# Four graph layers in one kernel: the transformer's weighing done for pairs of blocks, with both operands split into a rounded and a remaining part

## The chip, the cores and the metric

The kernel runs on one core of a Trainium2 chip. The metric is the device time of one execution in microseconds (us), smaller is better. TensorE is called PE below, its weight loads PEld, VectorE DVE, ScalarE ACT, GpSimd POOL, and SyncE, which issues the transfers, SP.

## The reference

A graph has 3125 nodes with 128 features each and 100000 edges. Four residual layers follow one another: a sum over neighbours with a small network, a convolution, an attention with four heads, and a transformer of four layers. The change concerns the last of them:

```python
h = x @ Wn + bn
for l in range(N_LAYERS):                      # 4
    Q = h @ WQ[l] + bQ[l]; K = h @ WK[l] + bK[l]; V = h @ WV[l] + bV[l]
    scores = jnp.sum(Q[dst] * K[src], axis=-1) * scale
    seg_max = jax.ops.segment_max(scores, dst, num_segments=n)
    e = jnp.exp(scores - seg_max[dst])
    seg_sum = jax.ops.segment_sum(e, dst, num_segments=n)
    attn = e / seg_sum[dst]
    messages = jax.ops.segment_sum(attn[:, None] * V[src], dst, num_segments=n)
    out = messages @ WO[l] + bO[l]
    h = _layernorm(h + out, ln_g[l], ln_b[l])
return h @ Wout + bout                         # added to x
```

## The kernel before

The kernel treats the edges as a dense matrix. Its first half (up to 1683 us of the trace) builds a 3125 x 3125 matrix of edge counts and, from it, a bias that is the logarithm of a pair's count and hugely negative where there is no edge, and runs the first three layers. The change leaves this alone. The transformer takes the rest.

3125 nodes are 25 tiles or blocks of T = 125. A row of 3125 columns is cut in NC = 7 chunks, four of 500 columns (four tiles) and three of 375 (three tiles). In each of the four layers (`layer`, called in a loop of three and once more with names that hold `last`) there are three stages, each a block of code that all engines begin and end together.

Ahead: `K`, `Q` and `V` are made by PE. `K` is split in a rounded part `k_high` (type float32r) and the rest, `k_low`. DVE adds V's bias and writes `vals` (L1643), which has a column of ones behind the 128 features, so that the weighing also gives the sum of the weights.

The attention loop runs over 25 blocks of 125 queries. For each block and chunk:

- `scores` (L1742): three PE products of float32r operands, q_high with k_low, q_low with k_high, q_high with k_high, into one of three PSUM banks. POOL makes q_high and q_low of a block.
- `maximum` (L1815): DVE adds the bias rows of the block, which SP loads two blocks ahead (L1694, 1.6 MB each), writes the sum into `row` and takes its maximum; after seven chunks it takes the maximum of these (L1821).
- `exponential` (L1786): ACT, in place in `row`.
- `turn` (L1760): PE turns each tile of 125 x 125 into a PSUM bank, four or three tiles to a bank, three banks in turn (class `Turned`).
- `turned.copy`: ACT (chunks 1, 3, 5, L1134) or DVE (the others, L1136) copies the bank to `wcol`.
- `weigh` (L1751): PE multiplies the turned weights of a tile, as the stationary operand, with that tile of `vals`, 129 columns, in plain float32. In the trace such a product is two records.
- `finish`: DVE takes the reciprocal of the sum and writes the message, queries by features.

The order on each engine is written by hand in `step`: at chunk c PE does the scores of the chunk two further on (`ahead`), which after the last chunk is one of a later block, the turn of chunk c, and the weighing of chunk c - 1. ACT and DVE follow in the same order; DVE takes the maximum that is due before it copies.

Behind: PE turns the message (L657), ACT copies it to `cols`, PE multiplies it with WO, giving rows (L675), DVE adds h (L1891) and takes the statistics of the normalisation, and DVE and ACT apply them (L119, L115). In the last layer POOL also adds the output's bias to x within the loop. The last stage multiplies with Wout and adds x.

## Time and profile before

| | us |
|---|---|
| median of three runs | 3273.34 (3272.65 to 3277.59) |
| the profiled execution, its own time | 3271.98 |
| its span, first to last instruction | 3270.2 |
| mean granted PE clock, share of full | 0.929 |

| engine | busy us | share of the span | instructions |
|---|---|---|---|
| PE | 2689.7 | 82% | 21697 |
| PEld | 2261.5 | 69% | 21697 |
| DVE | 2249.2 | 69% | 4979 |
| ACT | 1676.1 | 51% | 2854 |
| POOL | 228.0 | 7% | 510 |

The attention loops of the four layers begin at 1719.5, 2109.8, about 2500 and 2893.6 us. All times within the trace count from the span's start. A line number is that of the code that issued an instruction; the copies of turned banks have those of a helper (L1134, L1136). In the timeline a row gives start, duration, engine, line, operation, what it writes and reads, and in brackets the engine's idle time before it and what ended it; rows marked x4 or x8 merge neighbours of one kind. Matmuls overlap: the time from one start to the next, the pitch, is what one costs, and its duration holds the time to its end as well.

### The profile page before, as it was taken

To read this page: it belongs to the slowest core of one execution; us is meant where nothing else is said; L and a number is where in the kernel's file an instruction comes from. 1 tells how busy PE (TensorE), PEld (TensorE's weight loads), DVE (VectorE), ACT (ScalarE), POOL (GpSimd) and SP (SyncE) were. 2 spreads that over 40 slices of the span, in tenths; PEclk is the share of its full clock that TensorE was granted. 3 is DMA by queue.
4 is the path that set the end of the run, shared out by engine and by line. 5 is a ranking of instruction groups with operands and counts; after the bars stand their busy time and mean duration, and the time that the engine had idled before them with its cause. 6 is when DMAs were issued, how large, how long until landed. Compare 5 with 4: busy or idle time off the path is not lost. (4 is left out here: it accounts for less than half of the span.)

```text
span 3270.2 us, 63722 instructions
## 1 busy us (share of the span) xinstructions
PE 2689.7 (82%) x21697; PEld 2261.5 (69%) x21697; DVE 2249.2 (69%) x4979; ACT 1676.1 (51%) x2854; POOL 228.0 (7%) x510
## 2 busy tenths in 40 slices
PE   1788888755588888888739999799997999889997
PEld 0555555544466666666628999699986999779997
DVE  8999999635499998999775555455545555545555
ACT  1666666512288887888733444444443444344443
POOL 3000000000000000000001110011101111011110
PEclk9999999877789998899869999999998999999999
DMA  1232322651432335232113332133322333133331
GB/s 40 90 121 107 123 106 106 245 145 61 124 130 102 119 121 169 104 118 100 64 45 122 117 117 101 63 118 117 117 81 86 119 120 119 53 112 119 120 121 40
DMA packets 87027, 351.76 MB, mean 108 GB/s; under 512 B 47396, under 2 KB 59484, under 8 KB 59739
## 3 DMA queue, kind: packets, MB, share of 16 engines
q1 hardware_dynamic: 86841, 349.39, 30.6%
q8 instruction: 104, 1.70, 0.2%
q14 instruction: 82, 0.66, 0.1%
HBM read 284.26 MB, written 64.07 MB: 107 GB/s over the span
## 5 line engine op out<-in xcount | busy, mean ns | idle before, releaser
L1815 DVE CUSTOM_DVE_ANT_0 l_arow<-l_scores,abias 125x500 f32<-125x500 f32 (+1 forms) x525 | 325.3, 621 | 368.3 <-issue 311.5
L1751 PE MATMUL l_asum<-vals,l_awcol 125*125 125x129 f32 x3750 | 516.3, 277 | 34.5 <-DVE l_awcol L1136 34.2
L1751 PEld LDWEIGHTS l_asum<-vals,l_awcol 125*125 125x125 f32 x3750 | 454.6, 187 | 61.7 <-DVE l_awcol L1136 52.8
L1404 PE MATMUL gturned<-ident,grow 125*125 125x125 f32 x2500 | 411.1, 306 | 29.0 <-ACT grow L1342 29.0
L1404 PEld LDWEIGHTS gturned<-ident,grow 125*125 125x125 f32 x2500 | 333.7, 205 | 107.0 <-issue 73.1
L1134 ACT ACTIVATE l_awcol<-l_aturned 125x500 f32<-125x500 f32 (+1 forms) x225 | 122.7, 545 | 516.5 <-PE l_aturned L1760 516.5
L1311 DVE SCALAR_TENSOR_TENSOR grow<-line,a_dst 125x3125 f32<-125x3125 f32 x100 | 347.6, 3476 | 34.9 <-DMA line<-lines_dram 25.3
L1786 ACT ACTIVATE l_arow<-l_arow,l_aneg 125x500 f32<-125x500 f32 (+1 forms) x525 | 323.2, 658 | 81.0 <-DVE l_aneg L1821 81.0
L1320 DVE CUSTOM_DVE_ANT_0 grow<-grow,bias 125x3125 f32<-125x3125 f32 x100 | 341.6, 3416 | 23.9 <-DMA bias<-bias_dram 9.7
L1342 ACT ACTIVATE grow<-grow,neg 125x3125 f32<-125x3125 f32 x100 | 290.4, 2904 | 122.2 <-DVE neg L1323 122.2
L1382 PE MATMUL gparts<-gwcol,h_mem 125*32 125x125 f32 x5000 | 245.6, 292 | 109.3 <-ACT gwcol L1355 109.3
L1760 PEld LDWEIGHTS l_aturned<-ident,l_arow 125*125 125x125 f32 x1875 | 280.6, 187 | 23.2
L1355 ACT ACTIVATE gwcol<-gturned 125x1000 f32<-125x1000 f32 x300 | 281.7, 1001 | 16.3 <-PE gturned L1404 16.2
L1760 PE MATMUL l_aturned<-ident,l_arow 125*125 125x125 f32 x1875 | 289.0, 271 | 0.0
L1382 PEld LDWEIGHTS gparts<-gwcol,h_mem 125*32 125x32 f32 x5000 | 133.7, 114 | 166.3 <-ACT gwcol L1355 72.3
L1742 PE MATMUL l_scores<-k_low,l_q_high 128*125 128x500 f32 (+1 forms) x525 | 234.7, 447 | 9.4 <-POOL l_q_low L1715 6.7
L449 DVE TENSOR_SCALAR hot_key<-iota_key,fixed 128x325 bf16<-128x325 f16 x1000 | 240.8, 311 | 0.3 <-issue 0.3
L503 PE MATMUL win<-hot_key,hot_place 128*125 128x325 bf16 x750 | 138.8, 305 | 121.7 <-DVE hot_key L449 101.1
L503 PEld LDWEIGHTS win<-hot_key,hot_place 128*125 128x125 bf16 x750 | 90.1, 137 | 188.1 <-DVE hot_key L449 84.4
L564 ACT ACTIVATE blk<-win 125x325 f32<-125x325 f32 x250 | 96.8, 445 | 198.0 <-PE win L514 197.9
L1815 DVE CUSTOM_DVE_ANT_0 l_last_arow<-l_last_scores,abias 125x500 f32<-125x500 f32 (+1 forms) x175 | 108.5, 621 | 128.1 <-issue 105.0
L1136 DVE COPY l_awcol<-l_aturned 125x500 f32<-125x500 f32 (+1 forms) x300 | 182.9, 610 | 19.8 <-PE l_aturned L1760 19.8
(320 smaller groups left out, 4549.9 us busy)
## 6 DMA issues: line engine op xcount, KB each, us to landing
abias<-bias_dram SPq DMA_DIRECT2D x100, 1562.5 KB, 6.5
bias<-bias_dram SPq DMA_DIRECT2D x50, 1562.5 KB, 6.5
bias_dram<-lnrow SPq DMA_DIRECT2D x25, 1562.5 KB, 5.2
counts_dram<-pair SPq DMA_DIRECT2D x13, 1562.5 KB, 6.5
pair<-counts_dram SPq DMA_DIRECT2D x13, 1562.5 KB, 16.4
line<-lines_dram SPq DMA_DIRECT2D x8, 1367.2 KB
fixed<-kp SPq DMA_DIRECT2D x250, 4.0 KB, 1.7
agg<-counts_dram SPq DMA_DIRECT2D x2, 1367.2 KB
```

The lines of the kernel that those rows point to most:

```text
L449: last = dve.tensor_scalar(hot_key[p][:, i, keys], G["iota_key"][:, keys], fixed[r][:, k, i, 0:1], base, ALU.subtract, ALU.is_equal)
L1311: dve.scalar_tensor_tensor(out=row[n % RING][:, :], in0=line[g][:, 0, :], scalar=a_dst[:, b, k:k + 1], in1=line[g][:, 1, :], op0=ALU.add, ...
L1320: dve.tensor_tensor_reduce(out=here, in0=here, in1=bias[i % 2][0:T, :], scale=1.0, scalar=-3.0e38, op0=ALU.add, op1=ALU.max, accum_out=top ...
L1342: act.activation(row[n % RING][:, :], row[n % RING][:, :], ACT.Exp, bias=neg[:, b, k:k + 1], accum_out=den[:, b, k:k + 1]).then_inc(exp_do ...
L1355: act.activation(wcol[q % RING][:, :].rearrange("p (g n) -> p g n", g=2), bank[q % RING][:, :, 0:C4], ACT.Copy).then_inc(col_copied, 1)
L1382: last = pe.matmul(part_ps[CH * j:CH * (j + 1), at:at + T], vals[:, t, k, :], wcol[q % RING][:, (t - t0) * T:(t - t0 + 1) * T], start=(t < ...
L1404: last = pe.transpose(bank[q % RING][:, j // 4, j % 4 * T:(j % 4 + 1) * T], row[n % RING][:, t * T:(t + 1) * T], ident[0:T, 0:T])
L1742: last = pe.matmul(s_ps[c % S_BANKS][:, 0:z - a], left[p][:, :], right[:, a:z], start=(n == 0), stop=(n == len(terms) - 1))
L1751: last = pe.matmul(sum_ps[p][:, :], wcol[c % T_BANKS][:, j * T:(j + 1) * T], vals[:, t, :], start=(t == 0), stop=(t == NT - 1))
L1760: last = pe.transpose(bank[c % T_BANKS][:, j * T:(j + 1) * T], row[p][:, t * T:(t + 1) * T], ident[0:T, 0:T])
L1786: act.activation(row[p][:, a:z], row[p][:, a:z], ACT.Exp, bias=neg[p][:, :]).then_inc(exp_done, 1)
L1815: dve.tensor_tensor_reduce(out=row[p][:, a:z], in0=s_ps[c % S_BANKS][:, 0:z - a], in1=bias[p][0:T, a:z], scale=1.0, scalar=-3.0e38, op0=AL ...
```

## The change

The weighing is done for two blocks of queries at once, and the operands change sides: the values are the stationary operand and the turned weights are moved past them. Both are split into a rounded part of type float32r and the rest. `vals_high` meets the 250 rounded weights and the 250 remaining ones of a tile (512 columns with padding), `vals_low` meets the rounded ones (256 columns). The sum comes as features by queries, in two halves of a bank, which ACT and DVE copy and add into `cols`, so the turning of the message in the stage behind falls away.

A pair of blocks goes in 13 units of two tiles: four turns to a bank (two tiles of two blocks). ACT copies each bank rounded, then DVE subtracts and writes the rest (`low_part`), and PE may weigh. Three things stand out: `first` does 17 chunks of scores and maxima ahead, `ahead` is three chunks instead of two, and the last block goes alone in seven units.

The column of ones goes: ACT's exponentials sum themselves (`accum_out`), DVE adds the seven sums (`den`), and in the stage behind takes the reciprocal, multiplies by `has_in`, and scales each tile in the addition of h. Four rows of weights are held instead of two; they lie in the memory of x, in `agg` and in two new tensors. x is therefore stored to DRAM at the start of the transformer, with the output's bias already added by DVE, and loaded again in the last stage behind the last loop.

```diff
-        vals = sbo("vals3", [T, NT, D + 1])
+        vals_high = sbo("vals_high", [T, NT, D], FP32R)
+        vals_low = sbo("vals_low", [T, NT, D], FP32R)
+        row = [x[:, :, :].rearrange("p t d -> p (t d)")[:, 0:N], agg[0:T, 0:N], *(sbo(f"arow{k}", [T, N])[:, :] for k in range(2))]
+        wcol = [sbo(f"awcol{k}", [T, 2, 2 * HALF], FP32R) for k in range(T_BANKS)]
...
                 def _(sp):
+                    sp.wait_ge(x_made, 1)
+                    load_rows(sp, G["x_dram"], x[:, :, :].rearrange("p t d -> p (t d)"), loaded)
...
                 def _(dve):
+                    dve.wait_ge(first_in, 16 * 3)
+                    dve.tensor_tensor(x[:, :, :], x[:, :, :], bout[:, :].unsqueeze(1).broadcast_to([T, NT, D]), ALU.add).then_inc(x_made, 1)
...
+                            for c in range(NC):
+                                act.wait_ge(v_made, c + 1)
+                                act.activation(vals_high[:, part, :], spare[:, part, :], ACT.Copy).then_inc(v_rounded, 1)
...
+                            def low_values(c):
+                                dve.wait_ge(v_rounded, c + 1)
+                                dve.tensor_tensor(vals_low[:, part, :], spare[:, part, :], vals_high[:, part, :].bitcast(FP32),
+                                                  ALU.subtract)
                             for c in range(NC):
-                                dve.tensor_tensor(vals[:, ts[0]:ts[-1] + 1, 0:D], rows_view(bank, c, D),
+                                dve.tensor_tensor(spare[:, ts[0]:ts[-1] + 1, :], rows_view(bank, c, D),
...
+                                dve.wait_ge(v_made, c + 1)
+                                dve.sem_inc(banks.read["dve"], 1)
+                                if c:
+                                    low_values(c - 1)
+                            low_values(NC - 1)
...
+                    def ahead(P, e, u, act_on):
+                        for k in ((0, 1) if u == 0 else (u + 1,)):
+                            g = k + AHEAD
+                            to, f = (P + 1, 1 - e) if g < PAIR_CHUNKS else (P + 2, e)
+                            half, c = divmod(g % PAIR_CHUNKS, NC)
+                            if exists(to, half):
+                                act_on(to, f, half, c)
...
+                            def turn(P, e, u):
+                                pe.wait_ge(exp_done, (2 * P + halves - 1) * NC + (chunk_of(ts[-1]) + 1))
...
+                                for j, t in enumerate(ts):
+                                    for half in range(halves):
+                                        at = (halves * j + half) * T
+                                        last = pe.transpose(turned_ps[slot(P, e, u)][:, at:at + T], row[2 * e + half][:, t * T:(t + 1) * T], ident[0:T, 0:T])
+                                last.then_inc(turned_ready, 1)
+
+                            def weigh(P, e, u):
...
+                                pe.wait_ge(low_made, P * UNITS + (u + 1 + UNITS))
+                                wide = HALF if single(P) else 2 * HALF
+                                for j, t in enumerate(tiles(P, u)):
+                                    terms = ((vals_high, wide), (vals_low, HALF))
+                                    for n, (left, n_cols) in enumerate(terms if t == 0 else terms[::-1]):
+                                        last = pe.matmul(sum_ps[e][:, 0:n_cols], left[:, t, :], buffer[:, j * wide:j * wide + n_cols],
+                                                         start=(t == 0 and n == 0), stop=(t == NT - 1 and n == 1))
...
+                            def step(P, e):
+                                for u in units(P):
+                                    if not single(P):
+                                        ahead(P, e, u, scores)
+                                    turn(P, e, u)
+                                    if u:
+                                        weigh(P, e, u - 1)
+                                weigh(P, e, units(P)[-1])
...
+                                act.activation(row[k][:, a:z], row[k][:, a:z], ACT.Exp, bias=neg[k][:, :],
+                                               accum_out=expsum[k][:, c:c + 1]).then_inc(exp_done, 1)
...
+                            def step(P, e):
+                                for u in units(P):
+                                    act.wait_ge(turned_ready, P * UNITS + (u + 1 + 2 * UNITS))
+                                    act.activation(operand(P, e, u, 0), turned(P, e, u), ACT.Copy).then_inc(high_copied, 1)
+                                    if u == 1 and not (isinstance(P, int) and P == 0):
+                                        finish(P - 1, 1 - e)
...
+                                    for c in ((u + 2,) if u < 3 else (5, 6) if u == 3 else ()):
+                                        exponential(P, e, 1, c)
+                                    if 4 <= u < 4 + NC:
+                                        exponential(P + 1, 1 - e, 0, u - 4)
+                                    if u >= 4 + NC and exists(P + 1, 1):
+                                        exponential(P + 1, 1 - e, 1, u - 4 - NC)
...
+                            def low_part(P, e, u):
+                                dve.wait_ge(high_copied, P * UNITS + (u + 1))
+                                dve.tensor_tensor(operand(P, e, u, 1), turned(P, e, u), operand(P, e, u, 0).bitcast(FP32), ALU.subtract
+                                                  ).then_inc(low_made, 1)
+
+                            def finish(P, e):
+                                for half in range(1 if single(P) else 2):
+                                    dve.wait_ge(exp_done, b * NC + NC)
+                                    dve.tensor_reduce(den[:, bass.ds(b, 1)], expsum[k][:, :], AX.X, ALU.add)
+                                dve.wait_ge(msg_high, P + 1)
+                                dve.tensor_tensor(here, here, sum_ps[e][:, at:at + wide], ALU.add).then_inc(sum_read, 1)
+
+                            def step(P, e):
+                                for u in units(P):
+                                    if not single(P):
+                                        ahead(P, e, u, maximum)
+                                    low_part(P, e, u)
+                                    if u == 2 and not (isinstance(P, int) and P == 0):
+                                        finish(P - 1, 1 - e)
+                            first(maximum)
...
                         def _(pe):
-                            pe_turn(pe, banks, "msg", msg, D, ident)
-                            banks.done(pe, "msg")
                             pe_rows(pe, banks, "out", [cols], [w[:, 3, :]])
...
                         def _(act):
-                            act_columns(act, banks, "msg", cols)
                             norm.root(act)
...
                         def _(dve):
+                            chain(dve, m, dve.reciprocal(den[:, :], den[:, :]))
+                            chain(dve, m, dve.tensor_tensor(den[:, :], den[:, :], G["has_in"][:, :], ALU.mult))
...
-                                    dve.tensor_tensor(work[:, part, :], rows_view(bank, c, D), h[:, part, :], ALU.add).then_inc(banks.read["dve"], 1)
+                                    for j, t in enumerate(ts):
+                                        end = dve.scalar_tensor_tensor(out=work[:, t, :], in0=bank[0:T, j * D:(j + 1) * D], scalar=den[:, t:t + 1],
+                                                                       in1=h[:, t, :], op0=ALU.mult, op1=ALU.add)
+                                    end.then_inc(banks.read["dve"], 1)
```

## Rows read from the trace of the kernel before

**Rows 1.** The windows view, the loop of layer 1; busy us and instructions, then PE's clock.

```profile
core 0: us, PE busy (x) PEld busy (x) DVE busy (x) ACT busy (x) POOL busy (x), PEclk, DMA share, GB/s
1718.00:2060.00 342.00, 327.24 (x2401) 305.20 (x2401) 179.81 (x525) 140.20 (x251) 39.73 (x100) 1.00 0.31 109
```

**Rows 2.** The page's costliest groups: the weight loads of the weighing.

```profile
L1751 PEld LDWEIGHTS l_asum<-vals,l_awcol 125*125 125x125 f32 x3750 | 454.6, 187 | 61.7 <-DVE l_awcol L1136 52.8
```

**Rows 3.** The timeline, PE, one unit of the loop in layer 1.

```profile
1906.31 0.60 PE L1760 MATMUL l_aturned<-ident,l_arow 125*125 125x125 f32 x4
1906.63 0.96 PEld L1751 LDWEIGHTS l_asum<-vals,l_awcol 125*125 125x125 f32 x8
...
1906.74 1.05 PE L1751 MATMUL l_asum<-vals,l_awcol 125*125 125x129 f32 x8
...
1907.55 0.42 PE L1742 MATMUL l_scores<-k_low,l_q_high 128*125 128x376 f32 x1
...
1907.80 0.33 PE L1742 MATMUL l_scores<-k_high,l_q_low 128*125 128x376 f32 x1
...
1907.98 0.33 PE L1742 MATMUL l_scores<-k_high,l_q_high 128*125 128x376 f32 x1
...
1908.14 0.60 PE L1760 MATMUL l_aturned<-ident,l_arow 125*125 125x125 f32 x4
```

**Rows 4.** The timeline: the last score product of 500 columns, turns, ACT's copy.

```profile
1904.02 0.39 PE L1742 MATMUL l_scores<-k_high,l_q_high 128*125 128x500 f32 x1
...
1904.25 0.60 PE L1760 MATMUL l_aturned<-ident,l_arow 125*125 125x125 f32 x4
...
1904.88 0.59 ACT L1134 ACTIVATE l_awcol<-l_aturned 125x500 f32<-125x500 f32 x1 [4.80 <-PE l_aturned L1760]
```

**Rows 5.** The timeline: a block's last unit, where PE waits.

```profile
1900.14 0.49 PE L1760 MATMUL l_aturned<-ident,l_arow 125*125 125x125 f32 x3
...
1900.48 0.68 DVE L1815 CUSTOM_DVE_ANT_0 l_arow<-l_scores,abias 125x500 f32<-125x500 f32 x1 [0.99 <-issue]
...
1901.08 0.54 DVE L1136 COPY l_awcol<-l_aturned 125x375 f32<-125x375 f32 x1
...
1901.68 0.93 PE L1751 MATMUL l_asum<-vals,l_awcol 125*125 125x129 f32 x6 [0.39 <-DVE l_awcol L1136]
```

**Rows 6.** The timeline of ACT: a copy that sums, in the first half; exponentials.

```profile
416.33 0.59 ACT L577 ACTIVATE crow<-turn 125x500 f32<-125x500 f32 x1
416.79 0.21 ACT L577 ACTIVATION_READ_ACCUMULATOR crow<-turn 125x1 f32 x1
416.88 0.69 ACT L578 ACTIVATE lnrow<-turn,tiny 125x500 f32<-125x500 f32 x1
...
1911.22 1.31 ACT L1786 ACTIVATE l_arow<-l_arow,l_aneg 125x500 f32<-125x500 f32 x2 [0.86 <-DVE l_aneg L1821]
```

**Rows 7.** The timeline: stages behind the loop of layer 1 and ahead of the next.

```profile
2059.99 2.86 PE L657 MATMUL l_attn_out_bank<-ident,agg 125*128 125x125 f32 x25 [0.98 <-PEq L1687]
...
2063.86 5.72 PE L675 MATMUL l_attn_out_bank<-w,cols 128*125 128x128 f32 x50 [1.00 <-ACT cols L684]
...
2076.18 3.93 DVE L119 TENSOR_SCALAR h_mem<-work,stat 125x128 f32<-125x128 f32 x15 [0.15 <-DVE stat L106]
...
2102.97 0.69 DVE L1643 TENSOR_TENSOR vals<-l_qkv_bank,rows 125x512 f32<-125x512 f32 x1 [4.85 <-PE l_qkv_bank L675]
```

**Rows 8.** The timeline: the loop's start in layer 1 and in the last layer.

```profile
1719.52 0.49 PE L1742 MATMUL l_scores<-k_low,l_q_high 128*125 128x500 f32 x1 [2.24 <-POOL l_q_low L1715]
...
1720.76 0.68 DVE L1815 CUSTOM_DVE_ANT_0 l_arow<-l_scores,abias 125x500 f32<-125x500 f32 x1 [2.88 <-PE l_scores L1742]
...
1727.24 0.60 PE L1760 MATMUL l_aturned<-ident,l_arow 125*125 125x125 f32 x4
...
2893.56 0.78 PE L1742 MATMUL l_last_scores<-k_low,l_last_q_high 128*125 128x500 f32 x1 [7.02 <-POOL l_last_q_low L1715]
...
2902.54 0.60 PE L1760 MATMUL l_last_aturned<-ident,l_last_arow 125*125 125x125 f32 x4
```

**Rows 9.** The page's part on transfers: the bias rows, us from issue to landing.

```profile
abias<-bias_dram SPq DMA_DIRECT2D x100, 1562.5 KB, 6.5
```

245 lines of the change are left out of this document (111 added, 134 removed).

## The prediction

> **What bounds the kernel now.** I read the page's first two parts, then the windows by stage, then one unit of the attention loop in the timeline, since the change touches nothing ahead of the transformer. The windows show that in the loop over the 25 blocks of queries PE is busy for 327 of 342 us, its weight loads for 305, DVE for 180 and ACT for 140, and that its clock is granted in full, 2.4 GHz [rows 1]. The loop runs four times. In layer 1 it goes from the first score at 1719.52 to the end of the last block; the next PE work starts at 2059.99, so a layer's loop is 340.5 us, 7.7 of it ahead of the first turn at 1727.24 [rows 7, 8], and a block takes (340.5 - 7.7)/25 = 13.3 us.
>
> A unit of four tiles and 376 score columns lasts 1.83 us, from turn at 1906.31 to turn at 1908.14. Four turns take 0.43; eight weighing products (two a tile, since the operands are plain float32) take 0.81; a score product of 376 columns takes 0.17 to the next, one of 500 columns 0.23 (1904.02 to 1904.25) [rows 3, 4]; over several I read 0.171 and 0.227. So a turn is 0.108 us, a weighing tile 2 x 0.108. A block is 75 x 0.108 + 12 x 0.227 + 9 x 0.171 = 12.36 us of PE; the 13.3 leave 0.95 of gaps. The largest is at the last unit: DVE takes a maximum first, so its copy ends late and PE waits 0.39 [rows 5]. PE's own work sets the loop's time.
>
> **Weighing, the main term.** Two blocks now share one product. Per tile the rounded values meet 512 columns (both blocks, rounded and remaining part) and the remaining part of the values meets 256. Both are of the scores' type, whose pitch is 0.227 at 500 columns and 0.171 at 376, that is 0.45 ns a column: 0.232 at 512 and 0.117 at 256, 0.349 a tile. A pair of blocks falls from 100 x 0.108 = 10.8 to 25 x 0.349 = 8.7 us. Turns (50 x 0.108 = 5.4) and scores (8.5) stay. PE work of a pair: 22.6. The weight load of the next product must hide behind the 256-column one: the loads last 187 ns, but eight of them take 0.96, so they follow one another at 0.11 [rows 2, 3], hidden behind products of 0.108 now; so I cost them nothing; without that cover see rival 2.
>
> **The way from turn to weighing.** Today one engine copies a turned bank. Now ACT copies it rounded, DVE then subtracts and writes the rest, and PE waits for DVE. From the turns' last slot: 0.16 to their end (four turns last 0.60, their slots 0.43), 0.03 to ACT's start (1904.85 to 1904.88), 0.59 ACT, 0.03, 0.68 DVE (a sum of 512 from PSUM with a second operand lasts 0.69), 0.06 to PE as at 1901.62: 1.55 us [rows 4, 5, 7]. PE meanwhile weighs the unit before (0.70), scores (0.51 or 0.68) and turns (0.43): 1.64 to 1.81. The way is covered by 0.1 to 0.25, a thin cover. Gaps of a pair: the last unit has one tile, so 0.22 + 0.70 stands against a maximum (it starts 0.34 after the scores' last slot, 1900.14 to 1900.48, and takes 0.60 [rows 5]) and 0.46 for low part and signal, 0.5; the closing of the former pair on DVE (two sums of 0.16, one addition of about 0.4) shortly after the maximum's reduction, 0.3; the 0.03 a unit loses today, 0.4; the two double chunks, 0.3. Sum 1.5 us, between 0.5 (only the last unit) and 2.0 (today's, 2 x 0.95). A pair takes 24.1.
>
> **ACT and DVE.** ACT's exponentials now sum as well. Where ACT reads its accumulator today, the next instruction starts 0.09 after the read (416.79, 416.88), and a copy with its read takes 0.55, where a copy alone lasts 0.59 and overlaps its successor by 0.1 [rows 6, 4]; two exponentials last 1.31, so they follow at 0.61. A pair: 14 exponentials 9.1, 13 copies 6.2, closing 0.3: 15.6 of 24.1. DVE: 14 maxima 7.8, reductions 0.6, 13 subtractions 7.7, closing 0.7: 16.8 of 24.1. Neither is the bound. Behind DVE's new wait for ACT's copy stands the next maximum, and behind that PE's scores three chunks later; DVE is idle for a third of a unit, so nobody waits. Behind ACT's wait for the finished sum (unit 1) stand exponentials needed from unit 2 on, and the sum was finished a unit before.
>
> **The loop's ends.** Before the first turn now come 19 chunks of scores instead of 10, the 15th of which needs the bias rows of block 2. SP issues that load when the first chunk of block 1 has been read: first maximum 1.24 after the first score [rows 8], seven maxima about 4.2, one more 0.7, issue at 6.3; landing 6.5 later [rows 9], 12.8; one maximum, two chunks of scores: first turn at 14.8 instead of 7.7, with 9 x 0.61 = 5.5 of work moved ahead. The eleven full pairs take 265.1. In the pair before the last only four chunks of scores are left (2.1), PE has 16.2 of work and the way of 1.55 stands bare against 1.13 in ten units (4.2): 21.3 with the odd gap. The single block: 25 x (0.108 + 0.234) = 8.6 and seven gaps of 0.2, 10.0, then 0.7 for the sum's end. Loop: 14.8 + 265.1 + 21.3 + 10.7 = 311.9. That is 28.6 less than 340.5.
>
> **Ahead of the loop.** DVE adds V's bias at 0.69 a bank [rows 7], paced by PE at 0.875. Now each bank has a second operation of about 0.62, and the first must end before its bank is given back (0.05): 4 x 1.36 + 3 x 1.1 = 8.7 instead of 5.1 us, ACT's rounding hidden beside it. +3.7. The loop waits for it. PE idles for 6 us there instead of 2.2; in the last layer, where it idles 7.02, its first product lasts 0.78 instead of 0.49, which is the level of 1.2 GHz, and its first turn comes 8.98 after the first score instead of 7.72 [rows 8]. I take +1.2 for three layers (0 to 1.2).
>
> **Behind the loop.** 25 turns of the message and ACT's copies go: 2059.99 to 2063.86, -3.9. DVE's addition of h becomes 25 products with a column instead of 7 wide sums (priced like V's, 0.60 and 0.48 in pitch): 15 such operations on 128 columns took 3.93, 0.26 each [rows 7], up to 0.3 from PSUM, so 6.9 against 3.8, +3.1. The reciprocal of the sums and one product, on 25 columns each, fit before the first bank, 1 us after PE starts. Together -0.8, between -2 and +1.
>
> **Free of cost.** The addition of the output bias to x (3.5 us of DVE) lies in the node stage, where DVE waits while PE turns h and multiplies columns; SP's store of x waits for it, lands in about the 6.5 of an equally large load [rows 9], and that stage has 11 us left; SP has nothing queued behind. The reload of x lies beside 25 us of the last normalisation and costs 7 if that cover fails. GpSimd's memsets have 15 us. GpSimd's 25 additions to x go, off the path; its start in the last layer waits for four loads instead of five, perhaps -0.4, left out.
>
> **The sum.** Per layer -28.6 + 3.7 - 0.8 = -25.7, four times -102.8, and 3 x 1.2 = +3.6: -99.2. The profiled execution took 3271.98 (span 3270.2), 1.4 under the median of the three runs, 3273.34; from the median: 3174.
>
> **Rivals.** (1) The way through two engines sets the pace: PE turns the next unit only in name, and a bank's stay, 0.43 + 0.16 + 0.03 + 0.59 + 0.03 + 0.68 = 1.92, becomes the unit: 13 x 1.92 = 25.0 and 0.5 at the last, 25.5 a pair, +1.4 x 11.5 x 4 = +64, 3238. For it: the cover is only 0.1 thick and ACT, DVE have an order written out by hand. Against: three banks turn round, so a bank may stay for three units. The Trainium skill ("Trainium Kernel Development and Optimization", Best Practices) warns that speeding up TensorE does not speed up the emptying of PSUM; by that rule the change, which reads each bank twice, would end at this rival. The trace's 140 and 180 busy us of ACT and DVE leave room that the rule does not count, hence a low chance: 0.17.
> (2) The change does not do what it says: the product of 256 columns costs its weight load, 0.187 instead of 0.117, as PE can't hide a load behind so short a product of this type. +0.07 x 25 x 48 = +84, 3258. For it: no row has such a product. Against: loads of the same width follow at 0.11 in weighing [rows 3]. 0.10.
> (3) Slower: DVE's subtraction comes in behind a maximum that has just begun, and waits for 0.69 and the 0.17 of its start. The way becomes 1.55 + 0.86 = 2.41, and with one turn ahead the unit is half of 2.41 + 1.72 (PE's mean work), 2.07: a pair 27.4 with 0.5 at its end, +3.3 x 11.5 x 4 = +152, 3326. It is slower than before once a unit passes 1.98. For it: just this happens today at the last unit, where the copy waits for the maximum's end [rows 5]. Against: in other units the maximum is released 0.4 before the turn and ends 0.25 before ACT's copy. 0.07.
> (4) Gaps shrink to 0.5 a pair and the clock holds: -46 - 4, 3124. 0.12.
>
> **Chances.** Forecast 0.54 (3145 to 3210), the rivals as given. A measurement of this kernel can tell 0.2% (6.5 us) from no change. Faster 0.90, same 0.02, slower 0.08: rival 3, and the tail of 2. The range of 8 in 10 takes in rivals 1 and most of 4, and stops at rival 2's centre: 3128 to 3252.
>
> **What would show it.** Weighing at 0.232 and 0.117 in pitch, or 0.19 for the short one (rival 2). A unit of 1.64 to 1.85 with PE's idle time at weighing under 1.5 a pair, or PE waiting in each unit for DVE's low part (1, 3). First turn 14 to 15 us after the first score, DVE waiting there for the bias load. V's stage longer by 3 to 4, the stage behind shorter by 1. ACT and DVE busy 65% and 70% of the loop. Wrong would be the forecast if ACT's read of its accumulator costs its full 0.2 us in the exponentials (14 x 0.11 more, 17.1 of 24.1, still hidden, but unit 3 with two of them would stall), or if layers differ by more than the clock's 1.2.

## The result and the profile after

The changed kernel takes 3186.84 us (median; 3177.73 to 3191.4) against 3272.99 for the kernel before on the same chip: ratio 0.973, 95% interval 0.971 to 0.976, 86 us less. The forecast was 3174. The profiled execution took 3186.86, span 3185.1, 85.1 us shorter than the span before.

The windows view of the new kernel, over the loop of layer 1 (busy us and instructions by engine, then PE's clock), answers to [rows 1]:

```profile
core 0: us, PE busy (x) PEld busy (x) DVE busy (x) ACT busy (x) POOL busy (x), PEclk, DMA share, GB/s
1719.00:2030.00 311.00, 291.92 (x1742) 257.04 (x1740) 223.59 (x575) 207.86 (x523) 40.16 (x100) 0.99 0.34 120
```

PE is still busy for nearly the whole loop. DVE rose from 180 of 342 us to 224 of 311 (72%), ACT from 140 to 208 (67%).

The timeline of the new kernel, one unit (four turns, four weighing products, a chunk of scores, the next turns), answers to [rows 3, 4]:

```profile
1853.12 0.27 PE L1771 MATMUL l_aturned<-ident,agg 125*125 125x125 f32 x1
...
1853.15 0.36 PE L1783 MATMUL l_asum<-awcol,vals_low 125*128 125x256 f32 x1
...
1853.35 0.39 PE L1783 MATMUL l_asum<-awcol,vals_high 125*128 125x512 f32 x1
...
1853.43 0.59 ACT L1822 ACTIVATE awcol<-l_aturned 125x500 fp32r<-125x500 f32 x1 [0.55 <-PE l_aturned L1771]
1853.58 0.28 PE L1783 MATMUL l_asum<-awcol,vals_low 125*128 125x256 f32 x1
...
1853.70 0.40 PE L1783 MATMUL l_asum<-awcol,vals_high 125*128 125x512 f32 x1
...
1853.93 0.33 PE L1755 MATMUL l_scores<-k_low,l_q_high 128*125 128x376 f32 x1
...
1854.05 0.68 DVE L1862 TENSOR_TENSOR awcol<-l_aturned,awcol 125x500 fp32r<-125x500 f32 x1 [0.22 <-ACT awcol L1822]
...
1854.45 0.27 PE L1771 MATMUL l_aturned<-ident,x 125*125 125x125 f32 x1
```

The wide weighing product costs 0.23 (1853.35 to 1853.58, and 1853.70 to 1853.93), the short one 0.12 (1853.58 to 1853.70), to the next product's start. ACT's copy starts 0.04 after the last turn's end, DVE's subtraction 0.03 after the copy's, and it ends at 1854.73, when PE still has its turns to finish.

The pairs can be counted off by the one copy of the finished sum that ACT makes in each. The timeline of the new kernel, ACT alone, copies of pairs 1, 10, 11 and of the last block:

```profile
1771.96 0.38 ACT L1817 ACTIVATE cols<-l_asum 128x250 f32 x1
...
2013.77 0.38 ACT L1817 ACTIVATE cols<-l_asum 128x250 f32<-128x250 f32 x1
...
2032.17 0.38 ACT L1817 ACTIVATE cols<-l_asum 128x250 f32<-128x250 f32 x1
...
2041.87 0.28 ACT L1817 ACTIVATE cols<-l_asum 128x125 f32<-128x125 f32 x1 [1.65 <-PE l_asum L1783]
```

From the first to the second of these lie ten pairs: 24.18 us each.

To compare layers I take four marks from the timeline of each kernel: GpSimd's first operation of a layer, the first score, the first turn, and PE's first work behind the loop. In us, layers 1 to 4 (the last "behind" runs to the final stage's first product):

| stretch | before | after | change, all four |
|---|---|---|---|
| ahead: to the first score | 18.5, 23.3, 23.2, 25.1 | 22.7, 29.2, 29.0, 28.7 | +19.6 |
| first score to first turn | 7.7, 7.7, 9.2, 9.0 | 18.0, 17.1, 17.3, 16.8 | +35.6 |
| first turn to the loop's end | 332.8, 332.8, 333.0, 332.7 | 297.3, 297.4, 298.2, 298.1 | -140.3 |
| behind | 26.5, 26.4, 26.4, 24.4 | 25.2, 25.2, 25.1, 23.1 | -5.2 |

They add up to -90.3. The final stage has +1.4 and the unchanged first half of the program +3.8 in this execution; together -85.1. That first half varies: with the same code the first layer began between 1694.6 and 1715.1 us in the profiles below. Where an effect is small I therefore compare the time from the first layer's start to the end of the span: 1569.2 us before, 1480.3 after.

The timeline of the new kernel, the start of layer 1's loop, answers to [rows 8]:

```profile
1727.49 0.78 PE L1755 MATMUL l_scores<-k_low,l_q_high 128*125 128x500 f32 x1 [6.45 <-POOL l_q_low L1730]
1728.07 0.62 PE L1755 MATMUL l_scores<-k_high,l_q_low 128*125 128x500 f32 x1
1728.49 0.62 PE L1755 MATMUL l_scores<-k_high,l_q_high 128*125 128x500 f32 x1
...
1729.40 0.68 DVE L1852 CUSTOM_DVE_ANT_0 x<-l_scores,abias 125x500 f32<-125x500 f32 x1 [3.50 <-PE l_scores L1755]
...
1736.46 8.15 SPq L1709 DMA_DIRECT2D abias<-bias_dram  x2
...
1743.43 0.68 DVE L1852 CUSTOM_DVE_ANT_0 arow<-l_scores,abias 125x500 f32<-125x500 f32 x1 [3.39 <-DMA abias<-bias_dram]
...
1744.17 0.50 PE L1755 MATMUL l_scores<-k_low,l_q_high 128*125 128x500 f32 x1 [2.64 <-DVE l_atop L1852]
```

PE has idled for 6.45 us and its products follow at 0.42, not 0.23; DVE waits 3.39 us for block 2's bias rows, PE 2.64 for DVE. The granted clock of the first four microseconds says why the products are slow (windows view, new kernel):

```profile
1705.00:1715.00 10.00, 10.00 (x27) 4.98 (x28) 4.41 (x7) 7.63 (x13) 0.22 (x1) 1.00 0.83 322
...
1727.00:1731.00 4.00, 3.51 (x9) 2.80 (x10) 1.15 (x3) 0.74 (x1) 1.79 (x5) 0.50 0.29 68
```

Half of full speed, that is 1.2 GHz, after 6.45 us without work. The first four microseconds of the four loops were granted 0.50, 0.50, 0.51 and 0.59 in the new kernel, and 1.00, 1.00, 0.59 and 0.63 in the kernel before, where PE had idled 2.24, 2.25, 2.25 and 7.02.

In layers 3 and 4 the level fell once more behind the first turn (windows view, new kernel, the first 24 us from the first turn of layers 1 to 4):

```profile
1745.50:1769.50 24.00, 23.18 (x142) 20.64 (x141) 17.16 (x43) 16.38 (x41) 3.87 (x10) 1.00 0.52 192
2114.30:2138.30 24.00, 23.19 (x142) 20.63 (x141) 17.16 (x43) 16.38 (x41) 3.89 (x10) 1.00 0.53 191
2483.20:2507.20 24.00, 23.72 (x138) 21.36 (x137) 17.16 (x43) 16.49 (x41) 3.88 (x10) 0.93 0.50 180
2852.00:2876.00 24.00, 23.72 (x138) 21.42 (x138) 17.29 (x43) 16.48 (x41) 3.91 (x10) 0.93 0.49 178
```

These are the two loops that took 298.2 and 298.1 us in the table, some 0.8 more than the others.

The return from one layer to the next looks different too. The timeline of the new kernel, layer 2, answers to [rows 7]:

```profile
2068.01 0.45 POOL L1589 TENSOR_TENSOR rows<-rows 125x128 f32<-125x128 f32 x1 [72.17 <-POOLq L1956]
2068.23 2.70 SPq L1585 DMA_DIRECT2D abias<-bias_dram  x2
2071.05 0.15 DVE L1612 TENSOR_SCALAR bq<-bq 128x1 f32<-128x1 f32 x1 [8.01 <-issue]
...
2071.89 4.54 PE L665 MATMUL l_qkv_bank<-cols,w 128*128 128x500 f32 x5 [7.06 <-issue]
```

PE begins 3.9 us behind GpSimd, and the profile names nothing that it waited for. In the kernel before it began 0.2 behind.

### The profile page after: what moved, and what is told of

It reads as the page before. It is cut to its first block and busy times, and to the rows that moved or that the text cites. A ratio compares the mean times of both kernels' runs of the same rounds, so it can differ in the third digit from the quotient of the medians.

```text
span 3185.1 us, 60275 instructions
## 1 busy us (share of the span) xinstructions
PE 2573.7 (81%) x19197; PEld 2090.7 (66%) x19197; DVE 2451.7 (77%) x5292; ACT 1956.1 (61%) x3958; POOL 221.1 (7%) x487
## 5 line engine op out<-in xcount | busy, mean ns | idle before, releaser
L1822 ACT ACTIVATE awcol<-l_aturned 125x500 fp32r<-125x500 f32 (+2 forms) x489 | 279.2, 572 | 290.8 <-PE l_aturned L1771 288.8
L1365 PE MATMUL gturned<-ident,grow 125*125 125x125 f32 x2500 | 410.3, 306 | 29.2 <-ACT grow L1303 29.2
L1862 DVE TENSOR_TENSOR awcol<-l_aturned,awcol 125x500 fp32r<-125x500 f32 (+2 forms) x489 | 321.2, 657 | 109.9 <-ACT awcol L1822 102.1
L1365 PEld LDWEIGHTS gturned<-ident,grow 125*125 125x125 f32 x2500 | 332.8, 204 | 107.5 <-issue 73.0
L1783 PE MATMUL l_asum<-awcol,vals_high 125*128 125x512 f32 (+1 forms) x975 | 360.1, 390 | 19.0 <-DVE awcol L1862 19.0
L1281 DVE CUSTOM_DVE_ANT_0 grow<-grow,bias 125x3125 f32<-125x3125 f32 x100 | 341.7, 3417 | 24.4 <-DMA bias<-bias_dram 10.2
L1783 PE MATMUL l_asum<-awcol,vals_low 125*128 125x256 f32 x975 | 305.0, 322 | 13.5 <-DVE awcol L1862 12.9
L1316 ACT ACTIVATE gwcol<-gturned 125x1000 f32<-125x1000 f32 x300 | 282.0, 1002 | 19.2 <-PE gturned L1365 19.1
L1755 PE MATMUL l_scores<-k_low,l_q_high 128*125 128x500 f32 (+1 forms) x525 | 201.3, 383 | 27.5 <-POOL l_q_low L1730 19.3
L1783 PEld LDWEIGHTS l_asum<-awcol,vals_high 125*128 125x128 f32 x975 | 184.7, 189 | 43.2 <-DVE awcol L1862 18.8
L1852 DVE CUSTOM_DVE_ANT_0 arow<-l_scores,abias 125x500 f32<-125x500 f32 (+1 forms) x252 | 154.8, 622 | 74.5 <-PE l_scores L1755 56.8
L1783 PEld LDWEIGHTS l_asum<-awcol,vals_low 125*128 125x128 f32 x975 | 184.8, 190 | 31.8 <-DVE awcol L1862 30.0
L1755 PE MATMUL l_scores<-k_high,l_q_low 128*125 128x500 f32 (+1 forms) x525 | 194.0, 369 | 0.0
L1755 PE MATMUL l_scores<-k_high,l_q_high 128*125 128x500 f32 (+1 forms) x525 | 193.9, 369 | 0.0
```

The costliest lines, as they stand in the source:

```text
L1281: dve.tensor_tensor_reduce(out=here, in0=here, in1=bias[i % 2][0:T, :], scale=1.0, scalar=-3.0e38, op0=ALU.add, op1=ALU.max, accum_out=top ...
L1316: act.activation(wcol[q % RING][:, :].rearrange("p (g n) -> p g n", g=2), bank[q % RING][:, :, 0:C4], ACT.Copy).then_inc(col_copied, 1)
L1365: last = pe.transpose(bank[q % RING][:, j // 4, j % 4 * T:(j % 4 + 1) * T], row[n % RING][:, t * T:(t + 1) * T], ident[0:T, 0:T])
L1755: last = pe.matmul(s_ps[g % S_BANKS][:, 0:z - a], left[half][:, :], right[:, a:z], start=(n == 0), stop=(n == len(terms) - 1))
L1783: last = pe.matmul(sum_ps[e][:, 0:n_cols], left[:, t, :], buffer[:, j * wide:j * wide + n_cols], start=(t == 0 and n == 0), stop=(t == NT ...
L1822: act.activation(operand(P, e, u, 0), turned(P, e, u), ACT.Copy).then_inc(high_copied, 1)
```

## The experiments

My theory after reading: PE's own work sets the loop, the way over ACT and DVE is just covered, and the 13 us that the forecast missed lie at the seams (the bias wait, the stage ahead, the return to a layer's begin) and in the first half. The rivals: the way sets the unit; ACT or DVE is a bound; one of the seams is not what it seems. All edits are to the changed kernel, except where the heading names the kernel before.

**PE's work less: weighing without the values' remaining part.**

```diff
-  for n, (left, n_cols) in enumerate(terms if t == 0 else terms[::-1]):
+  for n, (left, n_cols) in enumerate(terms[:1]):
```

> Weighing keeps only the product of the rounded values; the product with the values' remaining part (256 columns, 0.117 us a tile) is left out, so the messages lack that part. My theory: PE's own work sets the unit, with a way from turn to weighing of 1.58 us just covered. Without two such products a unit has 1.49 of work; with one turn ahead it can't fall under (1.49 + 1.58)/2 = 1.53, so it goes from about 1.76 to 1.50 to 1.53: 2.3 to 2.9 us a pair, 46 pairs: 106 to 135 us less, some 3065 us. Rival (the way over ACT and DVE sets the unit, as a bank's stay of 1.9): 0 to 10 us less, 3180. Rival (the load of the next weights is not hidden behind the short product and costs 0.187): more than 150 less.

Measured: 3089.4 us, ratio to the kernel before 0.943 (0.939 to 0.946). From the transformer's start to the end 1383.9 instead of 1480.3, 96 less, where I expected 106 to 135. A pair takes 22.21 instead of 24.18 (ACT's copies of the sum, 1773.42 to 1995.50 for ten): -1.97, under the -2.3 expected. The time does follow PE's work, so the way alone is no bound; but the saving is 2.9 of PE's work and only two thirds of it came through. The timeline of this run, DVE with ACT's copies and one weighing product, says where it stops:

```profile
1877.26 0.68 DVE L1862 TENSOR_TENSOR awcol<-l_aturned,awcol 125x500 fp32r<-125x500 f32 x1 [0.22 <-ACT awcol L1822]
...
1878.06 0.68 DVE L1852 CUSTOM_DVE_ANT_0 arow<-l_scores,abias 125x500 f32<-125x500 f32 x1
...
1878.22 0.59 ACT L1822 ACTIVATE awcol<-l_aturned 125x500 fp32r<-125x500 f32 x1 [0.41 <-PE l_aturned L1771]
...
1878.85 0.68 DVE L1862 TENSOR_TENSOR awcol<-l_aturned,awcol 125x500 fp32r<-125x500 f32 x1
...
1880.67 0.51 PE L1783 MATMUL l_asum<-awcol,vals_high 125*128 125x512 f32 x1 [0.36 <-DVE awcol L1862]
```

DVE now goes from subtraction to maximum to subtraction with a gap of 0.22 or none. PE's waits for DVE in layer 1's loop rose from 27.1 us (60 times) to 35.0 (74 times) though PE had less to do. These rows suggest that DVE, together with the way, comes next, some 2 us a pair under today's; DVE was busy 208 of 272 us of this loop, so it isn't full, and no run parts the two.

**The way longer: ACT copies half of each bank once more.**

```diff
+  once = turned(P, e, u)[:, :, 0:T] if not single(P) else turned(P, e, u)
+  if u or not isinstance(P, int) or P:
+      act.wait_ge(high_copied, P * UNITS + u)
+  act.activation(extra[:, 0:once.shape[1], :], once, ACT.Copy)
   act.activation(operand(P, e, u, 0), turned(P, e, u), ACT.Copy).then_inc(high_copied, 1)
```

> ACT copies half of each turned bank (250 columns; all of it in the last block) once more, into a buffer of its own, ahead of its copy: the way from turn to weighing grows by about 0.38 us, PE's work stays. My theory (covered way, unit = the larger of PE's 1.72 and half of PE's 1.72 plus the way, now 1.96): a unit goes from 1.76 to about 1.84, 12 x 0.08 + 0.38 at the last unit = 1.3 us a full pair, 44 pairs; the pair before the last and the single block, where the way stands bare, +4.6 and +3.9 a layer: about +90 us in all, 3275. Rival (the way or the bank's stay is the unit): 0.38 x 12.5 x 46 = +220 us, 3405. Rival (a cover as wide as the three banks would allow, 1 us): only the bare places, +50.

Measured: 3300.3 us, ratio 1.007 (1.005 to 1.010): 115.6 us more from the transformer's start on, nearer to my +90 than to +220 or +50. The added copy lasted 0.38. A pair takes 26.38, +2.2 where I had +1.3, and the pair before the last 21.70 instead of 18.40. PE's waits for DVE in layer 1's loop more than doubled in number:

```profile
1880.39 0.38 ACT L1827 ACTIVATE extra<-l_aturned 125x250 f32<-125x250 f32 x1
...
1880.58 0.50 PE L1784 MATMUL l_asum<-awcol,vals_high 125*128 125x512 f32 x1 [0.81 <-DVE awcol L1868]
```

They are 57.3 us, 129 times, of 163 units. A kernel with 0.38 us more in the way is 0.7% slower than the one before the change: the cover is real and thin. The model (a unit is half of the way plus PE's work once the way is longer than PE's work) gives the right kind of answer and is 0.9 a pair low.

**The way shorter: DVE subtracts and writes half of each bank.**

```diff
-  dve.tensor_tensor(operand(P, e, u, 1), turned(P, e, u), operand(P, e, u, 0).bitcast(FP32), ALU.subtract
+  half = T if not single(P) else T // 2
+  dve.tensor_tensor(operand(P, e, u, 1)[:, :, 0:half], turned(P, e, u)[:, :, 0:half],
+                    operand(P, e, u, 0)[:, :, 0:half].bitcast(FP32), ALU.subtract
```

> DVE subtracts and writes only the first half of each bank's remaining part (the rest of it is left out of the result): the way is 0.3 us shorter, PE's work the same, DVE has 3.7 us less a pair. My theory (PE sets the unit): only the bare places gain, 0.3 x (11 last units + 12 units of the pair before the last + 7 of the single block) = 9 us a layer, 36 in all if every one of them is bare, 20 if half are: 3150 to 3167 us. Rival (the way sets the unit): 0.3 x 12.5 x 46 = 172 less, 3015. Rival (it doesn't matter at all): within 6 us of the changed kernel.

Measured: 3156.6 us, ratio 0.964 (0.961 to 0.967); 28.1 less from the transformer's start on. A pair takes 23.78 (-0.40, the last unit's gap and a little), the pair before the last 16.99 (-1.4). (DVE also has 3.7 us less to do in a pair here; this run doesn't part that from the shorter way.) The three runs fit together: PE's work less by 2.9 a pair gives 2.0; the way shorter by 0.3 a unit gives 0.4 a pair; the way longer by 0.38 a unit costs 2.2 a pair. In the changed kernel PE's work sets the full units and the way only the places where there is less work beside it.

**No sums in the exponentials.**

```diff
-  act.activation(row[k][:, a:z], row[k][:, a:z], ACT.Exp, bias=neg[k][:, :],
-                 accum_out=expsum[k][:, c:c + 1]).then_inc(exp_done, 1)
+  act.activation(row[k][:, a:z], row[k][:, a:z], ACT.Exp, bias=neg[k][:, :]).then_inc(exp_done, 1)
...
-  dve.tensor_reduce(den[:, bass.ds(b, 1)], expsum[k][:, :], AX.X, ALU.add)
```

> The exponentials no longer sum and DVE no longer adds up the partial sums (the division by the sums of weights is left out: divisor 1). My theory: ACT has a third of its time free, the 14 reads of its accumulator a pair (0.09 us each in pitch) and DVE's two reductions lie beside PE's work: 0 to 10 us less, of which the start of each layer's loop may give 1. Rival (ACT is the bound in the units with two exponentials, or DVE at the closing of a pair): 14 x 0.09 x 46 = 58 us less, 3129.

Measured: 3183.0 us, ratio 0.971 (0.968 to 0.974), and 1479.8 from the transformer's start against 1480.3. The sums of weights cost nothing that this measurement can tell.

**Block 2's bias loaded at the layer's start.**

```diff
+  sp.dma_start(row[2], G["bias_dram"][2, 0:T, :]).then_inc(bias2_in, 16)
...
+  added = row[2] if isinstance(P, int) and P == 1 and half == 0 else bias[half][0:T, :]
-  ... in1=bias[half][0:T, a:z],
+  ... in1=added[:, a:z],
```

(SP's loop leaves out its own load of that block.)

> The bias rows of block 2 are loaded at the layer's start into the buffer in which that block's scores with bias are written (free by then), so the 15th chunk of scores need not wait for a load that is issued after block 0 is read. My theory: DVE waited 3.4 us for that load in every layer, and PE with it; first turn 14.5 instead of 17.9 us after the first score, 4 x 3.4 = 14 us less, 3173 us. Rival (something else is as late, DVE's 19 maxima or ACT's 9 exponentials): under 1 us a layer, under 4 in all. Rival (three loads of 1.6 MB at the layer's start collide with what the first chunks need): no gain or a loss.

Measured: 3169.2 us, ratio 0.968 (0.966 to 0.970); 13.8 less from the transformer's start on. The first turn came 15.0, 14.3, 14.2 and 14.4 us after the first score, 11.4 less over the four layers, so most of the wait came back. Another 1.8 came in the loops of layers 3 and 4, which now took 297.3 and 297.2 us: the clock stayed at 1.00 over the first 24 us behind their first turns, where it had been 0.93.

**V made first.**

```diff
+  pe_rows(pe, banks, "v", [cols], [w[:, 2, :]])
   pe_columns(pe, banks, "k", w[:, 1, :], cols)
   pe_columns(pe, banks, "q", w[:, 0, :], cols)
-  pe_rows(pe, banks, "v", [cols], [w[:, 2, :]])
```

(ACT and DVE follow: V's rounding and bias first, five of the seven subtractions of V between those of K.)

> In the stage of the projections PE makes V first, then K and Q, so that DVE splits V beside PE's products for K and Q and not behind them; the work is the same. My theory: DVE's work of this stage is 14 x 0.65 + 7 x 0.74 = 14 us and bounds it only if it begins late; first score 18.5 to 19.5 us after PE's first product instead of 22.6, 3 to 4 us a layer, and PE idles less ahead of the scores, so that its clock stays at the upper level: another 0 to 1. 12 to 20 us less in all, 3170 us. Rival (ACT with 21 copies, or the block's end and GpSimd's staging, takes over): 0 to 4 less.

Measured: 3173.1 us, ratio 0.969 (0.967 to 0.971); 10.8 less from the transformer's start on, 2.7 a layer instead of 3 to 4 and more. The timeline of this run, the first score of layer 1:

```profile
1719.01 0.50 PE L1756 MATMUL l_scores<-k_low,l_q_high 128*125 128x500 f32 x1 [2.21 <-POOL l_q_low L1731]
1719.35 0.39 PE L1756 MATMUL l_scores<-k_high,l_q_low 128*125 128x500 f32 x1
```

PE's idle time is back at 2.21 us and the first products follow at the upper level, 0.34 and 0.23, but not for long: the first four microseconds of the four loops were granted 0.58, 1.00, 0.67 and 0.50. Of the clock's share little came back, and the short idle time alone doesn't keep the level. The first score comes 20.6 us after PE's first product instead of 22.6: PE waits for DVE within the stage now (0.76 and 0.35 in layer 1), and ACT waits for PE's products for Q.

Layer 2 of this run shows the new kernel's chain at the upper level: block 2's load was issued 6.7 us after the first score, DVE waited 3.38 us for it, and the first turn came at 15.7. In layers 1, 3 and 4, with the low level in the first four microseconds, the issue came at 8.1 to 8.9 and the first turn at 16.8 to 17.9.

**The same, by GpSimd.** V last as in the changed kernel, with GpSimd subtracting instead of DVE.

> The same stage with V last as in the changed kernel, but GpSimd makes V's remaining part, with DVE left to add the bias. An addition of 128 columns on GpSimd takes 0.45 us in this trace; no row shows one of 512. If it takes 1.0: first score 3 us earlier, 12 less in all. If it takes 1.6 (the length of four small ones without their start): 7 x 1.6 = 11 us against V's 6.1, no gain, 0 to +10.

Measured: 3189.6 us in one run, +2.8 from the transformer's start on. The timeline of this run, GpSimd:

```profile
1717.73 7.82 POOL L1594 TENSOR_TENSOR vals_low<-agg,vals_high 125x512 fp32r<-125x512 f32 x7 [12.71 <-ACT vals_high L1614]
```

Seven subtractions in 7.8 us: 1.27 for one of 512 columns and 0.99 for one of 384, between my two cases. The first score came only 0.1 earlier, since the last of them ends at 1725.55. What I had left out is that the seven take longer than PE's 5.6 for V, and that the chain (DVE's addition, ACT's rounding, GpSimd) also starts 2.5 us behind PE's first product for V.

**More code in a layer.**

```diff
   step(0, 0)
-  with eng.Fori(0, (LAST_PAIR - 2) // 2) as i:
+  step(1, 1)
+  step(2, 0)
+  with eng.Fori(1, (LAST_PAIR - 2) // 2) as i:
```

> Pairs 1 and 2 of each layer are written out instead of running in the loop: the same work, more instructions in a line. In layers 2 and 3 PE's first product stands 3.9 us behind GpSimd's start, waiting for nothing that the profile shows. Theory (instructions are fetched by DMA after the jump back to the layer's begin, and the more of them the program has the later they come): the wait at that place stays at 3.9 or grows, and new waits of the same kind appear inside the layer; 0 to +15 us. Rival (it is the bias loads that slow the stage's start): unchanged, 3.9, and total within 3 us.

Measured: 3176.3 us in one run, 1477.9 from the transformer's start on (-2.4). PE's wait at the return was 7.13 and 6.75, against 7.06 and 6.93, with 1037 matmuls in the code of a repeated layer instead of 753: it doesn't grow with the code.

**The bias loads later.**

```diff
   def _(sp):
+      sp.wait_ge(banks.filled, 1)
       for p in range(2):
           sp.dma_start(bias[p][:, :], G["bias_dram"][p, :, :]).then_inc(bias_in[p], 16)
```

> SP issues the two bias loads of a layer's start only when PE has filled its first bank, so that nothing else uses the DMA engines while PE's first instructions of the layer come. Theory (PE's start in layers 2 and 3 is late because its instructions are fetched by DMA and share the engines with 3.1 MB of bias): PE's wait before its first product falls from 7.0 to about 3.3 us, 7 us less in all. Rival (the fetch is late by itself, from the jump back on): the wait stays at 6.5 to 7.2 us.

Measured: 3183.9 us in one run, 1480.0 from the transformer's start on. The timeline of this run:

```profile
2068.70 3.70 PE L665 MATMUL l_qkv_bank<-cols,w 128*128 128x500 f32 x4 [6.94 <-issue]
...
2070.77 0.84 SPq L1586 DMA_DIRECT2D abias<-bias_dram  x2
```

With the loads issued 2.1 us behind PE's start, the wait is as long as ever (6.94 and 6.91). The bias loads are not its cause.

**The kernel before, with more code in a layer.**

```diff
-  with eng.Fori(0, NT // 2 - 1) as i:
+  with eng.Fori(0, 8) as i:
       step(2 * i, 0)
       step(2 * i + 1, 1)
-  for b in range(NT - 3, NT):
+  for b in range(16, NT):
```

> The kernel before, with blocks 16 to 21 of each layer written out instead of running in the loop: the same work, but 1059 matmuls stand in the code of a repeated layer instead of 633 (792 in the run without the values' remaining part, where PE began layers 2 and 3 without delay; 917 in the changed kernel, where it was 3.9 us late). Theory (the jump back to the layer's begin costs PE a fetch of instructions once its code for a layer is longer than something between 792 and 917 matmuls): PE's idle time before its first product in layers 2 and 3 rises from 3.3 to about 7 us, with the wait put down to issue, and the total by 7 to 8 us. Rival (it is something else in the changed kernel): 3.3, as in the kernel before.

Measured: 3270.6 us in one run, 1571.0 from the transformer's start on, against 1569.2. The timeline of this run:

```profile
2083.02 0.45 POOL L1615 TENSOR_TENSOR rows<-rows 125x128 f32<-125x128 f32 x1 [63.09 <-POOLq L1903]
...
2086.53 1.20 PE L665 MATMUL l_qkv_bank<-cols,w 128*128 128x500 f32 x1 [6.58 <-issue]
```

The wait is there (6.58 and 6.37 instead of 3.3), made by nothing but code written out: the late start belongs to the length of a layer's code. The expectation's counts are each 164 too high. The code of a repeated layer holds 469 matmuls in the kernel before, 628 without the values' remaining part, 753 in the changed kernel (39 for the projections, 51 ahead of the first turn, 142 for each of three pairs, 112 and 75 for the last two, 50 behind) and 895 here. So the limit lies above 628 and at most at 753.

The transfers of the profile show what goes with it. The part on transfers, changed kernel, layer 2 (2068 to 2437 us):

```profile
q8 instruction: 9, 0.15, 0.2%
```

Nine blocks of 16 KB came in on a queue that the profile names instruction, the first at 2069.0, 1.0 us behind GpSimd's first operation and 2.9 ahead of PE's first product. The run with more code has 11 of them in each of layers 2 and 3, this run 12. The kernel before and the run without the values' remaining part have none there, after 5 and 6 in layer 1, and in them PE is on time. So PE starts late where a layer's instructions are brought in anew at each repetition.

But it costs little. From GpSimd's first operation to the first score it is 24.0 us instead of 23.2 in both layers, since the kernel before has a stall of the same kind on DVE at that place, which the later start covers (timeline, kernel before):

```profile
2089.42 0.74 DVE L1637 SCALAR_TENSOR_TENSOR k_low<-l_qkv_bank,bq,k_high 128x500 fp32r<-128x500 f32 x1
...
2094.45 3.66 DVE L1637 SCALAR_TENSOR_TENSOR k_low<-l_qkv_bank,bq,k_high 128x500 fp32r<-128x500 f32 x6 [4.30 <-issue]
```

The run without the values' remaining part has the same: PE begins on time in layers 2 and 3, then waits 3.2 and 3.4 us for DVE, which is held up for 4.9 us (put down to issue), and the first score comes 28.0 and 29.6 us after GpSimd's first operation, against 29.2 and 29.0 in the changed kernel, where PE begins late: on average 0.3 apart. So my total of +7 to +8 was wrong while the wait was right, and I had read the wait as if all of it were a loss.

What does lengthen this stretch is the clock. The windows view over the 5.3 us from PE's first product on, first the changed kernel in layer 2, then the run without sums in layer 3, whose stage is the same:

```profile
2071.89:2077.19 5.30, 5.30 (x7) 2.32 (x8) 1.48 (x2) 1.35 (x2) 0.00 (x0) 0.50 1.01 419
...
2437.98:2443.28 5.30, 5.30 (x9) 2.38 (x10) 1.11 (x2) 2.16 (x4) 0.00 (x0) 0.71 1.00 417
```

At 0.50 the first score came 29.2 us after GpSimd's first operation, at 0.71 28.0.

**Both gains together.** Bias ahead and V first.

> Both edits that took time off: block 2's bias loaded at the layer's start, and V made first. By the traces of the two alone, the first turn came 2.7 us earlier after the first score in layers 1 to 4 with the one (15.0, 14.3, 14.2, 14.4 against 18.0, 17.1, 17.3, 16.8), and the first score 2.0, 1.1, 2.0, 2.8 us earlier after PE's first product with the other. If they add up: 11 + 8 = 19 to 24 us less than the changed kernel, ratio to the kernel before 0.9665 to 0.968. Rival (the two share a cover, since with V first the loads land later in relation to the scores): no better than the better one alone, 0.9677.

Measured: 3164.7 us, ratio to the kernel before 0.965 (0.962 to 0.968), below the changed kernel's interval of 0.971 to 0.976; 1456.3 from the transformer's start on, 24.0 less, where the two alone have 13.8 and 10.8. They add up. The first turn comes 14.4, 12.8, 12.8 and 15.2 us after the first score. The windows view of the first four microseconds of this run's loops in layers 2, 3 and 1:

```profile
2099.30:2103.30 4.00, 3.98 (x19) 3.23 (x19) 2.73 (x9) 0.28 (x1) 2.26 (x6) 1.00 0.29 63
2461.50:2465.50 4.00, 4.00 (x19) 3.24 (x20) 2.78 (x9) 0.23 (x1) 2.26 (x6) 1.00 0.27 59
1735.80:1739.80 4.00, 4.00 (x11) 3.21 (x12) 1.41 (x5) 0.24 (x1) 1.95 (x5) 0.57 0.36 82
```

With the same code and the same 2.2 us of idle time, the low level costs 1.6 us of this stretch (14.4 against 12.8). This is the fastest kernel of the study that computes the whole result.

## Why the prediction came out as it did

The time fell inside the range and 13 us above its centre; the mechanism was the one forecast.

- **Weighing.** 0.232 and 0.117 were read off the scores' pitch and stand in the trace, the short product as well. Rival 2 is out: the next weights' load hides behind 256 columns.
- **The pair and the loop.** 24.1 forecast, 24.18 measured; eleven pairs 266.0 (1745.48 to the turn at 2011.49) against 265.1. The pair before the last took 19.1, not 21.3, and the single block 12.2, not 10.7 (turns at 2011.49 and 2030.59, end at 2042.79). The first was costed as if the way stood bare in every unit, the second with gaps of 0.2 where PE idles up to 1.05; the two errors happen to cancel. First turn to the loop's end: 297.1 forecast, 297.3 in layer 1. All four: -140.3 against -142.8; 1.8 of the difference lie in layers 3 and 4, where the clock fell again behind the first turn.
- **The way.** 1.55 forecast; from the turns' last slot at 1853.23 to 1854.81 it is 1.58. Rivals 1 and 3 are out: in eleven full pairs of 13 units PE waits for DVE's part 43 times, 20.9 us in all, 1.9 a pair where the sum had 1.5 of gaps; in most units it doesn't wait, and DVE has finished its maximum and waits for ACT (0.22 in the unit above), not the other way round. What was said for rival 1, the thin cover, was right about its size (0.38 more made the kernel slower than before the change).
- **The Trainium skill's rule.** The Trainium skill ("Trainium Kernel Development and Optimization", Best Practices) says that "TensorE tiling speeds up compute but not PSUM evacuation", which the prediction took for a faster PE of any kind. Today's full units show little of it: with the way 0.3 a unit shorter a pair gained 0.4 of 24.2, and 28 us came back in all, in good part at the last units and the last pairs. The run with 2.9 us less PE work a pair, which gained 2.0, shows more of it.
- **Behind the loop.** -0.8 a layer forecast, -1.3 measured: eight products with a column took 2.16 from PSUM, 0.27 each, and DVE was otherwise covered as said.
- **Ahead of the loop.** +3.7 a layer forecast; +4.2 in layer 1, +5.9 in layers 2 and 3, +3.6 in the last. The extra 1.7 of layers 2 and 3 lies at the return to the layer's begin, a seam that I had not looked at. The run with the longer code before gives 0.7 of it for the same late start. The other 1.0 fits the clock: it stood at the low level for 5.3 us behind PE's start, against some 3 in the kernel before, and runs of the same stage in which that was some 3 too took 28.0 to 28.2 instead of 29.2.
- **First score to first turn: the mis-sized term.** 14.8 forecast, 18.0 measured in layer 1. The chain was right (block 2's bias, issued after block 1's first maximum, then one maximum, two chunks of scores), its first link was not: the issue came 9.0 us after the first score, not 6.3. PE was at 1.2 GHz, so that the first maximum began 1.91 after the first score instead of 1.24 and the first four followed at 1.1 to 1.25 instead of 0.6. The landing took 6.8, not 6.5, and DVE went on 0.2 later. At the upper level (V made first, layer 2) the issue came at 6.7 and the first turn at 15.7, so of the 3.2 us that layer 1 missed by some 0.9 are the chain itself and the rest goes with the clock.
- **The clock.** I gave it 1.2 in three layers, as a price of its own at the loop's start. But its low level stood inside the chain that I had timed from rows at the high one. Over four layers the stretch to the first turn grew by 35.6, against 28.4 plus the clock's 3.6. The 1.2 was small as well: the low level cost 1.5 in the kernel before (layers 1 and 2 against layer 3, 7.7 and 9.2) and 1.6 in the kernel with both gains.
- **The sum.** Ahead +4.8, first turn +3.6 (with the clock's share taken off), loop +2.5, behind -2.0: 8.9 of the 14.1 us by which the two profiles miss the forecast. The other 5.2 are the final stage (+1.4) and the first half (+3.8), whose code is the same. By layer the change is -22.3, -21.3, -22.2 and -24.5, where the forecast had -24.5 three times and -25.7. They differ by 3.2, more than the clock's 1.2, which the prediction had named as a sign of being wrong, and PE's idle time at weighing, 1.9 a pair where under 1.5 was named, is another.
- **The range.** It was said to take in most of rival 4, but begins at 3128, above that rival's 3124.
- **ACT's sums.** Said to be hidden, and hidden: 0.5 us of 1480 without them.

## What to carry to other kernels

When a loop runs two units deep over three engines, its steady pitch can be forecast closely from pitches of products of the same type (here 24.1 for 24.18); the error sat at its start, its end and between repetitions. Cost those seams as chains of their own, at the clock that PE will have after the idle time that the change itself makes, and in a range where the trace shows both levels after the same idle time. A wait that is put down to issue is not yet a loss: see what else would have stood there.

## What the runs showed of the hardware that I had not expected

- A layer repeated by a jump back began 3.3 to 4.0 us late on PE once its code was long: 469 and 628 matmuls gave 0.2, and 753, 895 and 1037 gave 3.9, 3.5 and 4.0 in layer 2. More code doesn't add to it, and putting off the bias loads doesn't take it away. It comes with 9 to 12 transfers of 16 KB on the queue named instruction in each repetition; in the kernels where PE was on time there were none.
- After 6.4 us without work PE's clock was granted at 0.50 to 0.51, that is 1.2 GHz, over the next 4 us in layers 1 to 3 of the changed kernel, and at 0.50 to 0.65 in the other runs with that idle time. After 2.2 us it was 1.00 in six loops and 0.57 to 0.67 in six others (layers 1 to 3 of the kernel before, the same with more code, the one with V first and the one with both gains), and what made the difference stays open.
- The read of ACT's accumulator is 0.18 to 0.21 us long in the rows, but takes 0.09 of ACT's time (1736.25 to the next exponential at 1736.34; without it exponentials of 500 columns follow at 0.61 instead of 0.70).
- GpSimd subtracts 512 columns in 1.27 us (1.23 from one to the next), where DVE takes 0.69 (0.61).
